# Graph layer on one core: the normalisation stage in another order, with more staging places

## The reference

```python
h = relu(layernorm(x))                                  # eps 1e-5
msg = concat([h[src], edges], -1) @ W_message           # (edges, 320) @ (320, 256)
agg = segment_sum(msg, dst)
v = layernorm(relu(agg) + h) * s0 + b0                  # eps 1e-6
u = relu_mlp_skip(v, W0, W1, W2)                        # three layers of 256 with skips
out = x + layernorm(h + u) * s1 + b1
```

## Time and profile before

| what | us |
|---|---|
| median of 3 timed runs | 2,143.26 (2,141.36 to 2,144.31) |
| the profiled execution: its span | 2,137.7 |
| busy: PE, VectorE, ScalarE, POOL | 1,634.1; 959.6; 400.6; 1,570.0 |
| gathers from h_table, POOL, 1,573 | 1,505.3 |
| gathers from x, POOL, 64 | 63.9 |

### The profile page before, as it was taken

The page is one execution under the profiler, slowest core; times in us unless marked ns, Lnnn a source line. Parts: engine busy times, 40 slices in busy tenths (PEclk is TensorE's granted clock), DMA queues, the critical chain, the costliest instruction groups (busy, mean ns, idle before and its releaser), DMA issues.

```text
span 2137.7 us, 41741 instructions
## 1 busy us (share of the span) xinstructions
PE 1634.1 (76%) x6722; PEld 1119.9 (52%) x6723; DVE 959.6 (45%) x4118; ACT 400.6 (19%) x1191; POOL 1570.0 (73%) x1645
## 2 busy tenths in 40 slices
PE   0169769669768867888887888888887887878887
PEld 0047547547546645555554555555554555555554
DVE  7865435345334434344343444343443433444436
ACT  4851112112111111111111111111111111111112
POOL 7457777777777777777777777777777777777773
PEclk9989889889889989999899989998999999999999
DMA  8995646656664664665566466466466466466462
GB/s 331 349 216 166 168 129 176 164 146 163 170 164 138 176 164 137 167 171 155 146 172 167 128 173 173 131 169 166 134 171 168 135 164 168 133 166 172 135 167 79
DMA packets 369198, 356.14 MB, mean 167 GB/s; under 512 B 256288, under 2 KB 312672, under 8 KB 369152
## 3 DMA queue, kind: packets, MB, share of 16 engines
q0 software_dynamic: 78576, 214.67, 35.5%
q1 hardware_dynamic: 232672, 88.13, 16.9%
q10 hardware_dynamic: 57904, 52.85, 8.0%
HBM read 329.01 MB, written 26.48 MB: 166 GB/s over the span
## 4 chain that ended last, share of the span: by engine, by line
POOL 44%; issue 21%; SPq 20%; PE 7%; DMA 3%; ACT 3%; DVE 2%; DVEq 0%; ACTq 0%; POOLq 0%
POOL ring L396 44%; SPq L365 14%; SPq L303 3%; PE acc_banks L562 3%; SPq L318 2%; DMA xs<-x 1%; ACT xs L693 1%; PE agg_bank L447 1%; ACT ring L693 1%; SPq L304 1%; DMA ring<-h_table,src_all 1%; PE agg_bank L452 1%; PE y_bank L435 1%; PE z_bank L435 1%; DMA visit_rows<-x 1%
## 5 line engine op out<-in xcount | busy, mean ns | idle before, releaser
L396 POOL DMA_INDIRECT ring<-h_table,src_all x1573 | 1505.3, 957 | 518.0 <-issue 477.0
L562 PE MATMUL acc_banks<-ring,onehot 128*128 128x320 f32 x3322 | 1065.1, 469 | 365.6 <-DMA ring<-h_table,src_all 227.2
L562 PEld LDWEIGHTS acc_banks<-ring,onehot 128*128 128x128 f32 x3322 | 642.4, 202 | 744.8 <-issue 557.2
L1091 DVE TENSOR_SCALAR onehot<-iota,dst_rel 128x128 f32<-128x128 f32 x1664 | 351.6, 297 | 297.5 <-PE acc_banks L562 278.6
L750 DVE TENSOR_TENSOR visit_rows<-agg_bank,visit_rows 128x256 f32<-128x256 f32 x98 | 41.6, 425 | 799.5 <-PE agg_bank L452 787.0
L610 ACT ACTIVATE uT<-z_bank,fp 128x128 f32<-128x128 f32 x196 | 78.9, 453 | 1277.0 <-PE z_bank L441 1277.0
L447 PE MATMUL agg_bank<-wm,ST 128*128 128x256 f32 (+1 forms) x582 | 170.5, 415 | 0.0
L447 PEld LDWEIGHTS agg_bank<-wm,ST 128*128 128x128 f32 (+1 forms) x582 | 110.8, 203 | 59.8 <-issue 40.5
L616 ACT ACTIVATE r_bank<-y_bank,fp 128x128 f32<-128x128 f32 x196 | 58.6, 337 | 292.9 <-PE y_bank L435 292.9
L452 PE MATMUL agg_bank<-wl,u 128*128 128x256 f32 x392 | 112.6, 410 | 0.0
L435 PEld LDWEIGHTS y_bank<-u,wl 128*128 128x128 f32 x784 | 104.7, 194 | 5.6 <-issue 0.3
(11 more groups left out here) (168 smaller groups left out, 1031.4 us busy)
## 6 DMA issues: line engine op xcount, KB each, us to landing
ring<-edges SPq DMA_DIRECT2D x208, 256.0 KB, 5.4
ring<-h_table SPq DMA_DIRECT2D x3072, 1.0 KB
ring<-h_table,src_all POOLq DMA_INDIRECT x1573, 4.6
xs<-x SPq DMA_DIRECT2D x14, 896.0 KB, 9.2
h_table<-xs SPq DMA_DIRECT2D x14, 896.0 KB, 5.7
h_in<-h_table ACTq DMA_DIRECT2D x98, 128.0 KB
visit_rows<-h_table ACTq DMA_DIRECT2D x98, 128.0 KB
visit_rows<-x ACTq DMA_DIRECT2D x98, 128.0 KB
```

The costliest lines, as they stand in the source:

```text
L396: nc.gpsimd.indirect_dma_start(out=ring[:, g % RG * G + j, 0:D], out_offset=None, in_=rows, in_offset=bass.IndirectOffsetOnAxis(ap=src_all ...
L562: return nc.tensor.matmul(acc_of(at), onehot[:, (k % OG) * G + j, :], ring[:, k * G + j, :], start=False, stop=True, skip_group_check=True)
L1091: op = nc.vector.tensor_scalar(onehot[:, ((k + AHEAD) % OG) * G + j, :], iota[:, :], dst_rel[:, bass.ds((g + AHEAD) * G + j, 1)], None, AL ...
```

## The change

- UNITS: a raw group follows every chunk from 5 to 11 and the last one follows chunk 13: chunks 0 to 5, raw 0, chunk 6, raw 1, chunk 7, raw 2, ... chunk 11, raw 6, chunks 12 and 13, raw 7. There are still eight raw groups (EG = 0, so the code for extra ones is empty).
- Chunks 0 to 3 are staged in the ring places of groups 4 to 7 (IN_RING = 4), the others in the five places of `xs`: nine places. Six chunks are asked for at once, three of them ahead of the two key tables. POOL gathers raw groups 4 to 7 when those chunks are stored.
- The key work of VectorE moves from after units 0, 1, 3, 4, 5 to after units 2, 4, 7, 10, 11, 12; the first one-hots to 14 and 16. On ScalarE it goes behind the steps 5, 6 and 8, each after `x_to_h(u - 1)`.
- `x_finish` stands before `second_layer`. The last visits' rows are loaded by SP after its main loop. `src` is loaded one chunk earlier.

```diff
-        if n < NX - 1 and (NX - n) % 2 == 0 and NX - n <= 6:
+        if n >= NX - 9 and n != NX - 2:
             UNITS.append(("raw", sum(kind == "raw" for kind, _ in UNITS)))
...
+        def staged(n):
+            if n >= IN_RING:
+                return xs[:, (n - IN_RING) % XS, :, :]
+            first = (RG - IN_RING + n) * G * F
+            return ring_flat[:, first:first + XB * D].rearrange("p (b d) -> p b d", d=D)
...
-            load_x(0)
-            load_x(1)
+            for n in range(3):
+                load_x(n)
             sp.dma_start(last_i[:, :], dst[P - 1:P, :].partition_broadcast(P)).then_inc(last_in, 16)
             sp.dma_start(dst_i[:, :], dst).then_inc(dst_in, 16)
-            for n in range(2, XS):
+            for n in range(3, AT_ONCE):
                 load_x(n)
             for n in range(NX):
-                s = n % XS
                 sp.wait_ge(h_ready, n + 1)
-                sp.dma_start(h_rows[:, n * XB:(n + 1) * XB, :], xs[:, s, :, :]).then_inc(h_stored[s], 16)
-                if n in (NX - 4, NX - 2):
-                    load_edges((n - NX + 4) // 2, 0, (n - NX + 4) // 2 + 1)
-                if n == NX - 3:
-                    load_src(src_in, RG, NG)
-                if n >= 1 and n - 1 + XS < NX:
-                    sp.wait_ge(h_stored[(n - 1) % XS], 16 * ((n - 1) // XS + 1))
-                    load_x(n - 1 + XS)
+                sp.dma_start(h_rows[:, n * XB:(n + 1) * XB, :], staged(n)).then_inc(h_stored[buffer_of(n)], 16)
+                if n + AT_ONCE < IN_RING + XS:
+                    load_x(n + AT_ONCE)
+                elif IN_RING + XS <= n + 3 < NX:
+                    sp.wait_ge(h_stored[buffer_of(n + 3)], 16 * (use_of(n + 3) - 1))
+                    load_x(n + 3)
+                if n == NX - 4:
+                    load_src(src_in, RAWS, NG)
+                if n in (NX - 3, NX - 2):
+                    load_edges(n - NX + 3, n - NX + 3, n - NX + 4)
...
+            for k in range(RG):
+                pool.wait_ge(group_free, k + 1)
+                if k >= RG - IN_RING:
+                    pool.wait_ge(h_stored[k - RG + IN_RING], 16)
+                gather(k, k, x, [raw_in[k]] * PAIRS)
...
+            keys = {5: blocks_of_tiles, 6: destinations, 8: wrong_keys}
             x_root(0)
-            act.wait_ge(dst_in, 16)
-            nc.scalar.activation(dst_f[:, :], dst_i[:, :], ACT.Copy).then_inc(dst_ready, 1)
-            for u in range(1, len(UNITS)):
+            x_to_h(0)
+            x_root(1)
+            for u in range(2, len(UNITS)):
                 x_root(u)
...
                 x_to_h(u - 1)
+                if u in keys:
+                    keys[u]()
...
-            parts = {0: cast_iotas, 1: check_keys, 3: relative_keys, 4: closing_places, 5: steering}
+            parts = {2: cast_iotas, 4: shift_lasts, 7: check_keys, 10: relative_keys, 11: closing_places, 12: steering,
+                     14: lambda: first_onehots(0), 16: lambda: first_onehots(1)}
             for u in range(len(UNITS)):
-                if u == EARLY:
...
                 x_moments(u)
-                if u < EARLY and u in parts:
+                if u in parts:
                     parts[u]()
-                if u == 0:
-                    shift_lasts()
+            x_finish()
             second_layer()
-            x_finish()
```

More of the change, by code:

```diff
@@ L239, in build @@
         keys_ready = sem("keys_ready")
-        raw_in = [sem(f"raw_in{k}") for k in range(RG)]
+        raw_in = [sem(f"raw_in{k}") for k in range(RAWS)]
         raw_ready = sem("raw_ready")
@@ L246, in build @@
         edges_in = [sem(f"edges_in{k}") for k in range(RG)]
+        extra_edges_in = [sem(f"extra_edges_in{e}") for e in range(EG)]
         group_free = sem("group_free")
@@ L357, in _ @@
+            for s in range(IN_RING + XS):
+                sp.wait_ge(h_stored[s], 16 * USES[s])
+            for e in range(EG):
+                load_extra_edges(e)
+            for i in range(1, MID + 1):
+                sp.dma_start(row_src[:, i, :], src[0:1, :, i * RT + RT - 1 + EG * G], allow_slow_non_contiguous=True).then_inc(row_src_in, 16)
+            sp.wait_ge(row_src_in, 16 * MID)
             row_regs = registers(nc.sync, BY_ROW)
@@ L393, in _, with gather @@
             nc.gpsimd.iota(block_start_i[:, :], pattern=[[P, NB]], base=0, channel_multiplier=0).then_inc(iotas, 1)
-            def gather(g, rows, semaphores, count=G):
+            def gather(g, k, rows, semaphores, count=G):
                 for j in range(count):
                     nc.gpsimd.indirect_dma_start(
-                        out=ring[:, g % RG * G + j, 0:D], out_offset=None, in_=rows,
+                        out=ring[:, k * G + j, 0:D], out_offset=None, in_=rows,
                         in_offset=bass.IndirectOffsetOnAxis(ap=src_all[:, g, j:j + 1], axis=0),
@@ new lines, in landed @@
+            def landed(k):
+                return gathered[k * PAIRS:(k + 1) * PAIRS]
+            pool.wait_ge(raw_src_in, 16)
+            for k in range(RG):
+                pool.wait_ge(group_free, k + 1)
+                if k >= RG - IN_RING:
+                    pool.wait_ge(h_stored[k - RG + IN_RING], 16)
+                gather(k, k, x, [raw_in[k]] * PAIRS)
+            for e in range(EG):
+                gather_extra(e)
+            pool.wait_ge(src_in, 16)
+            for s in range(IN_RING + XS):
+                pool.wait_ge(h_stored[s], 16 * USES[s])
@@ L415, in _ @@
+            for g in range(RAWS, NG):
+                k = (g - RAWS) % RG
+                pool.wait_ge(group_free, g + 1 - (EG if g < RAWS + RG else 0))
+                by_row = k == RG - 1 and g < NG - TAIL
+                gather(g, k, h_table, landed(k), ENDS if g == NG - 1 else G - 1 if by_row else G)
             pool.wait_ge(tables, 1)
@@ L419, in _ @@
                     for g in range(NG):
-                        freed = nc.gpsimd.compute_val(p * NG + g + 1)
+                        freed = nc.gpsimd.compute_val(p * NG + g + 1 + LATE)
                         pool.wait_ge(src_in, 16)
                         pool.wait_ge(group_free, freed)
-                        gather(g, h_table, landed(g))
+                        gather(g, g % RG, h_table, landed(g % RG))
                 nc.gpsimd.nop()
@@ L568, in close @@
                     sel = steered[VSEL]
-                    rhs = ring[:, bass.ds(at + k * G, 1), :].rearrange("p a f -> p (a f)")
-                    nc.tensor.matmul(acc_of(sel), close_hot[:, :], rhs, start=False, stop=True,
+                    closing = rhs[:, bass.ds(at + k * G, 1), :].rearrange("p a f -> p (a f)")
+                    nc.tensor.matmul(acc_of(sel), close_hot[:, :], closing, start=False, stop=True,
                                      skip_group_check=True).then_inc(block_closed, 1)
@@ L592, in _ @@
                 group(0, 0, k, "raw")
-            with nc.Fori(1, ROUNDS - 1, engines=[mybir.EngineType.PE], hint_back_edge=True) as i:
+            for e in range(EG):
+                group(0, 0, e, "extra")
+            with nc.Fori(1, MID + 1, engines=[mybir.EngineType.PE], hint_back_edge=True) as i:
                 for k in range(RG):
                     group(0, i, k, "SP")
-            for k in range(RG):
-                group(0, ROUNDS - 1, k, "last", ENDS if k == RG - 1 else G)
+            for k in range(TAIL):
+                group(0, MID + 1, k, "tail", ENDS if k == TAIL - 1 else G)
             with nc.tensor.If(passes < 2):
```

173 lines of the change are left out of this document (99 added, 74 removed).

## The result

The changed kernel takes 2,149.82 us (median of 6 runs, 2,145.92 to 2,150.84), the kernel before, timed beside it, 2,142.31 (6 runs, 2,140.56 to 2,144.31). The ratio is 1.0032, with a 95% interval of 1.0022 to 1.0042. By this ratio the kernel is slower by 6.9 us, with 4.7 to 9.0 as the interval; the forecast was 5.6.

What follows compares the result with a forecast made beforehand. POOL's unbroken gathers after the restart bound the kernel; + 11.2 us to the last chunk's normalisation, - 6.1 behind it and + 0.5 for visit rows give + 5.6: 2,143.3 + 5.6 = 2,148.9 us, range 2,142 to 2,153.5.

Steps and rivals of the forecast that it cites:

- What bounds it: Main loop: POOL issues gathers without a stop from 144.78 us, so whatever moves that point moves the end equally.
- the restart: POOL's third h_table group, after waiting for PE to free group 2: forecast to go from 144.8 to 150.4 us.
- T' = 118.6: First stage: time the last chunk is normalised after the change, 107.4 before; forecast + 11.2 us.
- the wait in raw 2: First stage: VectorE, three statistics into raw group 2, waits for ScalarE's roots of chunk 7, from 55.8 until 59.6.
- The wait for chunk 3: First stage: VectorE waits 4.2 us for chunk 3, which stands behind the two key tables in the queue.
- the walk: The forecast's step-by-step timing of VectorE and ScalarE through the first stage's changed order of units.
- 0 to 4: End of the first stage: 0 to 4 us added where VectorE and ScalarE wait for each other.
- row_bank at T' + 10.2: Behind the last chunk's normalisation: row_bank runs when the parameters land, where it was 16.3 behind; gains 6.1 us.
- The 0.5 for the visit's rows: Behind row_bank: visit 0's rows of h and x come late; between 0 and 2 us lost, 0.5 taken.
- 5.6 us around the span: Measurement: the timed median 2,143.3 is 5.6 above the profiled span 2,137.7, taken as what lies around it.
- Rival A: First stage becomes compact, VectorE's sum alone counts: last chunk normalised at 103.8, restart 135.1, time 2,133.6 us; 12%.
- Rival D: Main loop: SP's row loads pace the run, the start doesn't matter; + 0 to + 2 us, within another rival's 26%.

Runs made afterwards that it cites:

- e10: The kernel before with only the new order of units and of a visit's two steps: 2,143.74 us, ratio 1.0003 to the kernel before.
- e6: The changed kernel with the key work early again on VectorE and ScalarE: 2,147.31 us, ratio 1.0016 to the kernel before.
- e8: The changed kernel without the four ring places, five chunks asked for at once: 2,164.95 us, ratio 1.0099 to the kernel before.
- e5: The changed kernel with three raw groups ahead of the last chunk, as before, not seven: 2,147.37 us, ratio 1.0019 to the kernel before.
- e11: The changed kernel with five raw groups ahead of the last chunk, parameters and row_bank early, key work early: 2,140.77 us, ratio 0.9990 to the kernel before.
- e1: The changed kernel with three raw groups ahead of the last chunk, run at the slow pace: 3,607.55 us, ratio 1.0035 to the kernel before.
- e9: The changed kernel with the parameters loaded behind chunk 9's store, not the last chunk's: 2,146.18 us, ratio 1.0016 to the kernel before.

## Why the prediction was right

- **What bounds it.** Right. In the eight kernels the restart moves the end one to one, as closely as the intervals of about 2 us each way can tell, and from restart to last gather it is between 1,962 and 1,967 us in every profile.
- **T' = 118.6.** Measured 119.05. The check of the keys ended at 48.15 (forecast 47.2), the wait in raw 2 was 3.58 us until 60.4 (3.8, until 59.6), the end of the stage was ScalarE's: its units stand without a gap from 103.8 to 119.0, and the roots of raw 7 in front of the last chunk cost only their own 0.2 us (between 115.30 and 115.50). The wait for chunk 3 was 2.6, not 4.2. Two waits for roots were not in the walk, 2.28 at 15.65 and 1.43 at 38.51. The first has the same cause that I used for raw 2: ScalarE gives chunk 1's roots only when it has normalised chunk 0. The walk had 12.5 us of waits, the trace has 17.6, and the "0 to 4" at the end that I set at 1.5 was not there. Chunk 13 was not asked for 14 us ahead of need either: its load was issued at 100.21 and VectorE was ready for it at 105.9 and waited 0.7. That T' came within 0.5 is in part luck: such errors stood against each other.
- **Behind T: row_bank at T' + 10.2.** Measured 11.9. I took the landing of the last parameter load from before, 6.1 us; it was 8.5, in e10 8.3, in e6 9.4. The gain was thus 4.4 and not 6.1 (e10 4.6, e6 3.5). This is the term that was mis-sized most. Why the landing takes longer no run shows; before, nothing waited for it. The 0.5 for the visit's rows was wrong in sign: from row_bank to the restart it was 0.5 less. Sum + 6.75 against + 5.6.
- **5.6 us around the span.** Wrong in what it is. In this and the seven profiles of that pace the profiled execution's own time is 1.5 to 1.8 above its span, and 2,145.92 is the lowest of its six. Before's span and 1.8 make 2,139.5, under all six of its runs, so most of the 5.6 was a profiled execution quicker than the others. The sum is not touched, since it adds a difference to the median.
- **Rival A, the compact stage.** The Trainium skill's rule beside it (Trainium Kernel Development and Optimization, Best Practices: double-buffer so that transfers overlap compute) was open; for this case the runs answer it. Nine places in place of five bring 13.5 us of T in the changed kernel (e8), but in e10, with early keys, the tables ahead and before's rule of asking, five leave only 2.7 us of waits for chunks. And e5 waits 18.6 us for them with nine. So more places did not make the stage compact; work between the chunks fills the waits. How late SP asks for the next chunk adds to them, by the rows of e5, e8 and e11.
- **Rival D.** Rightly small at this pace, and the whole story at the other (e1).
- **What of the 11.7 us is whose.** Along e10, e6 and the changed kernel: the order of the units 6.4; all else but the key work (nine places, the tables behind three chunks, SP's rule of asking, the later first one-hots) 2.1; the late key work 3.2. By another way it splits otherwise (e8, e11), so these are no prices of single edits.

## What to carry to other kernels

When an engine runs without a stop from some point to the end, find that point and what it hangs on; here every microsecond of it is one of the time. Moving independent work into a place where an engine waits costs only what is left over (in e10 6.4 of VectorE's 14.8 us), so look for the wait first and then for the work; and a helper that gives roots one unit ahead also hands its lateness to the next engine. Behind the critical store, ask what is queued on which engine without having to be: the parameters alone moved the restart by 5.0 us (e9), where the whole new order of the units moved it by 1.6 (e10). And when places are added, ask when each is filled again: a free place that nobody asks for is worth nothing.

## What the runs showed of the hardware

- The same kernel ran in 2,143 and in 3,594 us, on one and the same chip. In the longer runs TensorE's mean granted clock is 0.74 (e1) and in the shorter 0.92 (the changed kernel); whether as a cause or as a consequence no run shows. In the longer runs instructions that are short otherwise took far longer at times: the issues of SP's row loads have a median of 228 ns in both profiles, but reach 1,409 ns where they never pass 312. First the rows of e1, then those of the changed kernel:

```profile
L401 SPq DMA_DIRECT2D ring<-h_table x3072: 2/228/1409, 262.0 to 3516.5; - x192
```

```profile
L401 SPq DMA_DIRECT2D ring<-h_table x3072: 224/228/312, 187.6 to 2034.3; - x192
```

- From the issue of the last chunk's store to the first gather behind it, it was 4.8 to 6.2 us in nine profiles, and 20.3 to 20.5 more for the 16 gathers where nothing else held them.
